# A one-core transformer block: the first half's attention ahead of all other work, the second half's scores behind two feed-forward units

## What is computed

```
h = layernorm(x) * (1 + ca) + sa
# latent attention: kv_latent = h W_to_kv^T (64), c = kv_latent W_compress^T (32), ch = layernorm(c)*gamma+beta
q, k, v = ch Wq^T, ch Wk^T, ch Wv^T          # one head of 32; rotary embedding on q and k
attn = softmax(causal(q k^T / sqrt(32)))      # 1024 x 1024
z = (attn v) W_comp2lat^T;  x = x + ga * (z (W_to_kv + W_out_res^T) + b_out)
h = layernorm(x) * (1 + cb) + sb
# gate, up: 2048 x 256, down: 256 x 2048, weights as packed 4-bit codes with one scale per 32
x = x + gb * ((gelu(h Wg^T) * (h Wu^T)) Wd^T)
```

## Time and profile before

| | us |
|---|---|
| median of 3 runs | 216.76 |
| lowest, highest | 214.21, 218.32 |
| the profiled execution, its own time | 217.49 |
| its span, first to last instruction | 215.5 |

### The profile page before, as it was taken

How to read it: one execution, slowest core, us unless ns; L and a number is a source line. 1 busy time by engine, 2 the same in 40 slices (tenths; PEclk the granted TensorE clock), 3 DMA queues, 4 the chain that set the end, 5 groups by cost and what they waited for, 6 DMA issues and landing times. The chain is left out here.

```text
span 215.5 us, 3087 instructions
## 1 busy us (share of the span) xinstructions
PE 198.3 (92%) x1064; PEld 159.3 (74%) x1064; DVE 142.7 (66%) x267; ACT 90.8 (42%) x151; POOL 59.4 (28%) x52
## 2 busy tenths in 40 slices
PE   7899998999769969989999999999899999999991
PEld 2496476574446848878898889887698889889891
DVE  0665995878799999999999844945832333323235
ACT  2011141642478526437535556354243542552420
POOL 4404043515152620200000000463342633624200
PEclk9885895599999999999999999999999999999998
DMA  5999675400000000000000000000200000000002
GB/s 177 324 349 235 193 230 196 171 4 3 0 0 2 0 0 3 2 0 0 3 0 0 3 0 0 0 0 5 97 2 0 0 0 0 3 0 0 0 0 97
DMA packets 5644, 11.30 MB, mean 52 GB/s; under 512 B 544, under 2 KB 2752, under 8 KB 5632
## 3 DMA queue, kind: packets, MB, share of 16 engines
q1 hardware_dynamic: 5216, 10.82, 16.0%
q10 hardware_dynamic: 416, 0.33, 0.6%
HBM read 10.09 MB, written 1.05 MB: 52 GB/s over the span
## 5 line engine op out<-in xcount | busy, mean ns | idle before, releaser
L866 PE MATMUL ps<-H,WS 128*128 128x512 f32 x384 | 94.7, 394 | 3.6 <-DVE wmod_sb L714 2.8
L866 PEld LDWEIGHTS ps<-H,WS 128*128 128x128 f32 x384 | 69.6, 188 | 18.9 <-DVE wmod_sb L714 4.3
L866 PEld LDWEIGHTS ps<-WS,IS 128*128 128x128 f32 x384 | 49.8, 191 | 3.8 <-issue 1.7
L866 PE MATMUL ps<-WS,IS 128*128 128x256 f32 x384 | 50.9, 283 | 1.1 <-DVE wmod_sb L714 0.9
L429 ACT ACTIVATE IS<-wmod_sb 128x512 fp32r<-128x512 f32 x32 | 20.3, 634 | 64.1 <-PE ps L866 41.0
L284 DVE TENSOR_TENSOR IS<-wmod_sb,IS 128x512 fp32r<-128x512 f32 x32 | 22.1, 690 | 26.6 <-ACT IS L429 25.0
L293 POOL TENSOR_TENSOR WS<-wbuf,WS 128x1024 fp32r<-128x1024 f32 x10 | 24.2, 2421 | 50.3 <-ACT WS L410 50.3
L714 DVE TENSOR_TENSOR wmod_sb<-ps,wmod_sb 128x512 f32<-128x512 f32 x32 | 22.0, 688 | 22.7 <-PE ps L866 20.7
L298 POOL TENSOR_TENSOR WS<-wbuf,WS 128x512 fp32r<-128x512 f32 x10 | 13.7, 1371 | 38.4 <-ACT WS L417 38.4
L423 ACT ACTIVATE wmod_sb<-ps 128x512 f32<-128x512 f32 x32 | 18.7, 586 | 6.2 <-PE ps L866 6.2
L866 PE MATMUL ps<-idle 128*128 128x512 bf16 x46 | 16.3, 502 | 1.3 <-POOL idle L487 1.3
(11 more groups left out here) (116 smaller groups left out, 203.3 us busy)
## 6 DMA issues: line engine op xcount, KB each, us to landing
wbuf<-packed SPq DMA_DIRECT2D x8, 384.0 KB, 17.7
wbuf<-scales SPq DMA_DIRECT2D x8, 384.0 KB
xres<-x SPq DMA_DIRECT2D x2, 512.0 KB, 6.2
wmod_sb<-wmod SPq DMA_DIRECT2D x1, 1024.0 KB, 11.0
out<-xres SPq DMA_DIRECT2D x4, 256.0 KB, 2.2
wmod_sb<-wmod SPq DMA_DIRECT2D x1, 512.0 KB, 7.1
rope_sb<-rope SPq DMA_DIRECT2D x1, 512.0 KB, 12.0
cst<-consts SPq DMA_DIRECT2D x1, 322.0 KB, 5.3
```

Of the source, the lines that this page charges most:

```text
L866: return pe.matmul(o, lhsT, rhs, start=start, stop=stop)
```

## The change

Every list of the front is written anew; what is computed stays the same.

- *Transfers.* x, with the identity matrix in front, comes as one tensor `head` laid out by partition, half 0 first; wmod likewise in two contiguous parts. SP's order is head half 0, wmod's first third, head half 1, the rest of wmod, consts, then rope half 0, group 0, rope half 1, group 1 and so on.
- *First LayerNorm.* `norm1` is gone. x is transposed raw; the mean is taken out in the weights (`wcm` minus 1/256 of its column sum, which PE computes in `weight_sum`), and 1/std is applied in `compress`, which also loses one step (eps sits in a 33rd column of `csq`).
- *Moved between engines.* `gamma_beta` and the sb and cb columns go from VectorE to ScalarE, the copy of xnT's second half too; both gate floors and `gab` go from VectorE to GpSimd; two of half 0's four `norm2` tiles go to ScalarE; staging of H for half 0 is split over both. `norm2` writes rows unpermuted, and `transpose2` reads with a step of 2.
- *Half 0.* Row scores come largest piece first, each with a bank of its own, and `max_rows(0)` follows each maximum. cb, sb and gb products, `project_c(1)` and `transpose_c(1)` are put in between on PE. The residual and the statistics alternate by tile; one reciprocal serves four tiles.
- *Feed-forward first.* `gate_up(0)` and `gate_up(1)` stand before half 1's row scores, `down(0)` behind the first four of these, `gate_up(2)` behind the other four, then half 1's key blocks without a unit in between, then `down(1)`. ScalarE does gelu of units 0 and 1 before half 1's exponentials. Unit 0, not unit 1, uses banks 2 and 3. `add_bias(1)` goes behind half 1's key blocks.
- *Fillers.* `stay_warm` has 10 matmuls at the start for 14, then 3, 2 and 4 in all that follow for 3, 4, 3, 2, 3, 3, 10 and 4.

```diff
@@ SP
+            sp.dma_start(head[:, 0:first], x[:, 0:first]).then_inc(x_in[0], 16)
+            sp.dma_start(wmod_flat[:, 0:KT * 2 * D], wmod[:, 0:KT * 2 * D]).then_inc(wmod_in[0], 16)
+            sp.dma_start(head[:, first:], x[:, first:]).then_inc(x_in[1], 16)
+            sp.dma_start(wmod_flat[:, KT * 2 * D:], wmod[:, KT * 2 * D:]).then_inc(wmod_in[1], 16)
             sp.dma_start(cst[:], consts).then_inc(cst_in, 16)
...
@@ ACT
             norm1_out(0)
             spread(0)
+            act.wait_ge(ga_done, 1)
+            act.activation(ga_b[:], bank(WO_B)[:, D:2 * D], ACT.Copy).then_inc(ga_out, 1)
+            norm1_out(1)
+            gamma_beta(0)
             v_high(0)
             qk_high(0)
             spread(1)
...
             exps(0, 0, HT)
+            split_d(0, 0)
+            out_high(0)
...
+            gamma_beta(1)
+            split_gu(0, 0)
+            v_high(1)
...
             spread(2)
+            norm2_h0((2, 3))
+            stage_h0()
             qk_high(1)
+            for n in range(2):
+                gelu(n, n, False)
+                inter_hi(n, n, False)
+                (split_gu, split_d)[n](1, 1)
             spread(3)
             max_rows(1)
+            exps(1, 0, 2 * HT)
...
@@ POOL
+            rsqrt(N_LN1)
             pool.wait_ge(a64_in, 16)
...
             rsqrt(N_LN1 + 1)
             rsqrt(N_LNC)
+            pool.wait_ge(ga_out, 1)
+            gate_floor(ga_b[:], ga_b[:]).then_inc(ga_ready, 1)
...
             add_bias(0)
             rsqrt(N_LNC + 1)
+            low_d(pool, 0, 0, 0)
             low_gu(pool, 0, 0, 0)
             rsqrt(N_LN2)
+            pool.wait_ge(gb_out, 1)
+            pool.wait_ge(wo_ready, 1)
+            gate_floor(gb_b[:], gb_b[:]).then_inc(gb_ready, 1)
+            low_gu(pool, 1, 1, 1)
+            low_d(pool, 1, 1, 1)
             for b in range(1, 2 * HT, 2):
                 probs_low(pool, 1, b, b + 1)
+            add_bias(1)
...
@@ DVE
             compress(0)
+            dve.tensor_copy(cbias[:], bank(SA_B)[:, DC:2 * DC]).then_inc(cbias_ready, 1)
+            decode(0, 0, 1)
             normc(0)
+            decode(0, 1, 3)
             rotate(0)
...
             split_qk(0)
+            row_max(0, 0, HT)
+            compress(1)
+            decode(0, 3)
...
+            aggregate(0, N_LN2)
             rotate(1)
...
+            norm2(0, (0, 1))
+            stage_h0()
             split_v(1)
             split_qk(1)
+            decode(1, 1, 3)
+            inter_full(0, 0, False)
+            inter_low(dve, 0, 0, False)
             decode(1, 3)
+            inter_full(1, 1, False)
+            inter_low(dve, 1, 1, False)
+            row_max(1, 0, HT)
+            decode_more(0, 1)
+            row_max(1, HT, len(pieces(1)))
+            for b in range(0, 2 * HT, 2):
+                decode_more(min(4, 1 + b // 2), min(4, 2 + b // 2))
+                probs_low(dve, 1, b, b + 1)
...
@@ PE
+            pe.wait_ge(ca_ready, 1)
+            weight_sum(bank(SUM_B, DC), M_CA).then_inc(sum_done, 1)
+            mod_columns(bank(SA_B, KT), SA, False).then_inc(moda_done, 1)
+            project_c(0, 0, HT)
...
+            transpose1(1)
+            stay_warm(0, 3)
             transpose_c(0)
+            project_c(1, 0, 2)
             project_qkv(0)
             stack_qk(0)
+            project_c(1, 2, HT)
+            scores(0, 0, HT)
+            max_rows(0)
             stay_warm(0, 2)
             key_scores(0, 0, 0)
             key_scores(0, 1, 1)
             key_scores(0, 2, 2)
+            pe.wait_ge(var_ready[N_LNC + 1], 1)
+            mod_columns(bank(MODB_B)[:, M_SB:M_SB + KT], SB, True)
             attend(0, 0, 0)
...
+            mod_columns(bank(MODB_B)[:, M_CB:M_CB + KT], CB, True).then_inc(modb_done, 1)
+            transpose_c(1)
+            output(0)
...
             project_qkv(1)
+            stay_warm(7, 4)
             stack_qk(1)
+            transpose2(0)
+            gate_up(0, 0, 0, 0, 0, first=True, later=False)
...
+            gate_up(1, 0, 0, 0, 1, later=False)
+            scores(1, 0, HT)
+            down(0, 0, 0, 0, 0, first=True)
+            scores(1, HT, len(pieces(1)))
+            gate_up(2, 1, 0, 1, 0)
             max_rows(1)
             for b, k in blocks(1):
                 key_scores(1, b, k)
                 if b >= 2:
                     attend(1, b - 2, k - 2)
...
+            down(1, 0, 0, 0, 1)
```

More of the change, by code:

```diff
@@ L65 @@
 EARLY = 2
-STEPS_AT_START = 5
-H0_BLOCK = 4
+STEPS_AT_START = 4
 H1_UNIT = 12
@@ new lines, in _ @@
+            dve.wait_ge(ca_ready, 1)
+            link(dve.tensor_tensor(wcm[:], wcc[:], mods[:, M_CA:M_CA + KT].unsqueeze(2).to_broadcast([P, KT, DC]),
+                                   ALU.mult))
+            dve.wait_ge(sum_done, 1)
+            dve.scalar_tensor_tensor(wcm[:], bank(SUM_B, DC).unsqueeze(1).to_broadcast([P, KT, DC]), -1.0 / D, wcm[:],
+                                     ALU.mult, ALU.add).then_inc(wcm_ready, 1)
+            dve.wait_ge(x_in[1], 16)
+            for i in range(HT, TILES):
+                bn(i)
@@ L797, in _ @@
-            probs_low(dve, 0, 3, HT)
-            decode(1, 2, 3)
-            out_stack(0)
-            rotate(1)
+            probs_low(dve, 0, 2, HT)
+            decode(1, 0, 1)
+            out_stack(0)
+            softmax_sums(0)
+            residual1(0, 0)
+            for i in range(HT):
+                if i < HT - 1:
+                    residual1(0, i + 1)
+                dve.wait_ge(x1_ready, i + 1)
+                bn(i)
+            aggregate(0, N_LN2)
+            rotate(1)
+            dve.wait_ge(rstd_ready[N_LN2], 1)
@@ new lines, in _ @@
+            inter_low(dve, 1, 1, False)
[5 more added lines that the diff above has]
+                probs_low(dve, 1, b, b + 1)
+            for n in range(2, UNITS + 2):
+                G = n // 2 + 1
+                if n == 2:
+                    dve.wait_ge(wgu_lo, 2)
+                    dve.wait_ge(wd_lo, 2)
+                    low_gu(dve, G, G % 2, G)
+                inter_full(n, n % 2)
+                if n == 2:
@@ L900, in _ @@
             pe.wait_ge(idle_ready, 1)
-            stay_warm(WC_B, 14)
+            stay_warm(WC_B, 10)
+            transpose1(0)
             pe.wait_ge(a64_in, 16)
@@ L1023, in gate_up @@
                     pe.wait_ge(wgu_lo, G + 1)
[L1024 to L1033 removed]
+                products = ((0, 0), (1, 0), (0, 1))
+                both = [(m, q) for m in range(2) for q in range(3)]
+                if first:
+                    both = [(m, q) for q in range(2) for m in range(2)] + [(m, 2) for m in range(2)]
+                for m, q in both:
+                    a, b = products[q]
+                    if later and q == 0:
+                        pe.wait_ge((gelu_done, inter_done)[m], n)
+                    if first and b and m == 0:
+                        pe.wait_ge(h_lo, 2 * (h + 1))
+                    for k in range(2):
+                        last = mm(bank(banks[m]), WS[:, par, a, k, m, P * e:P * (e + 1)], H[:, h, b, k, :],
+                                  q == k == 0, q == 2 and k == 1)
+                    if q == 2:
+                        last.then_inc((gate_done, up_done)[m], 1)
             def down(n, G, h, par, e, first=False, last=False, any_h=None):
@@ L1120, in _ @@
                 d = n - 2
-                down(d, d // 2, d // UNITS, d // 2 % 2, d % 2, first=d % UNITS == 0, last=d == UNITS - 1)
+                if d > 1:
+                    down(d, d // 2, d // UNITS, d // 2 % 2, d % 2, first=d % UNITS == 0, last=d == UNITS - 1)
             with pe.Fori(0, 3) as it:
```

497 lines of the change are left out of this document (233 added, 264 removed).

## The result

The changed kernel takes 224.02 us (median of 4 runs, 223.05 to 226.97); the kernel before, on the same chip, 216.70 (214.21 to 218.32). The ratio is 1.036, 95% interval 1.024 to 1.049: **slower**, outside the predicted range. The profiled execution took 223.54 us, its span is 221.7.

What follows compares the result with a forecast made beforehand. PE's and VectorE's chains to gate_up(12) were taken as the bound; PE's gave 4.75 us, VectorE's the deciding 4.2, so 217.5 - 4.2 = 213.3, less 0.7 for the median, rounded to 212.5 us; range 207.5 to 218.

Steps and rivals of the forecast that it cites:

- Part 1: Start to half 0's key scores: without LayerNorm's normalisations and with reordered transfers, done at 30.75, 6.1 us ahead.
- Part 2: Half 0's key scores to its output: output at 37.6, 8.6 us ahead, at the full clock.
- Part 3: Half 0's output to the first units: gate_up(0) at 46.9; units 0 and 1 done where unit 0 had 14 us to go.
- Part 4: Half 1's attention: 4.7 us PE wait, first exp at 68.0 (before 58.60), gate_up(4) at 83.2, 3.85 us ahead.
- the clock falls in the gap: Rival, chance 0.20: clock falls in Part 4's 4.7 us gap, gate_up(2) takes 5.5 instead of 2.8, gain 1.5, 215.3 us.
- Part 5: inter_full(3) to inter_full(11): VectorE takes 34.9 us, so gate_up(12) comes 4.2 us earlier.
- Slower: Rival, chance 0.11: clock stays low through half 1's attends, 219.1 us, or 222 with half 0 low too.
- hold between VectorE and GpSimd: In Part 4: exclusive lock for instructions with two SBUF inputs, not for PSUM readers; without it 1.5 us shorter.

Runs made afterwards that it cites:

- e1_decode_ahead: The changed kernel with decode steps 1 to 5 of the later groups done before half 1's first probability (STEPS_AT_START 6 for 4): 219.48 us.
- mended order: The changed kernel with decode two steps ahead and gelus of units 0 and 1 before split_gu(1,1); with fillers 215.13, repeated 0.994; without 218.66, repeated 1.014.
- w1_scores_first: The changed kernel with half 1's row scores ahead of the units, decode two steps ahead, gelus behind all exponentials, gb floor late: 216.09 us, ratio 0.991.
- w2_scores_first_trimmed: w1_scores_first with split_gu(1,1) behind half 1's exponentials, low_gu(1,1) on VectorE, gb floor back in the row maxima: 212.45 us, ratio 0.987.
- w4_scores_first_warm_early: w2_scores_first_trimmed plus eight fillers before max_rows(1) and five in the wait for the first attention bytes: 210.16 us, ratio 0.971.

## Why the prediction was wrong

The forecast and the profiled execution at the same points (us; the last column is how late the kernel was against the forecast):

| | forecast | measured | late |
|---|---|---|---|
| key scores of half 0 | 30.75 | 31.62 | 0.9 |
| output of half 0 | 37.6 | 39.56 | 2.0 |
| `gate_up(0)` | 46.9 | 50.25 | 3.4 |
| `gate_up(2)` | 62.3 | 65.73 | 3.4 |
| first exp of half 1 | 68.0 | 72.91 | 4.9 |
| `gate_up(4)` | 83.2 | 88.81 | 5.6 |
| `gate_up(12)` | 117.2 | 127.48 | 10.3 |

*Part 1 was right in its steps.* The first attention bytes landed 0.8 later than assumed, and `project_c(0)` ran at half clock, 3.60 us for my 2.6; of that 0.9 of lateness was left at the key scores.

*Part 2 and Part 3 were right in their steps and off in the clock.* The attends of half 0 at half clock I had priced (2.5 to 3.5 later) and not taken; by the output 1.1 of lateness came to the 0.9. `stack_qk(1)` took 3.47 us where I had the 1.98 of the earlier trace rows, nearly all of the next 1.4. GpSimd's floor of gb took five steps of 0.72 to 1.08 us, 4.6 in all for my 3; it ended at 49.8, before anything waited for it.

*Part 4 was right in its shape:* the gap of 4.7 us came as 4.41, VectorE's decodes and the split behind it in the order described, the two extra table loads with 1.28 each. Its term for `gate_up(2)` and for the attends was at the full clock, against 4.25 us and a clock of 0.66 measured. The rival "the clock falls in the gap" came true, but it priced one place, at 2.7 us, and 1.4 were lost there. The clock fell in at least three (at `stack_qk(1)`, in the gap, after the first attend). That the two falls after 60 us come with the waits is what the fillers show. For the first it is less sure: in e1_decode_ahead's profile `stack_qk(1)` stood behind the same wait of 0.88 us and took 1.96. The Trainium skill ("TensorE: Matmul & The Clock Gate", Part 1, "What's actually happening") has the throttled clock as the default and activity as what releases it; the runs agree for the holes after 60 us (1.00 with both filled, 0.50 to 0.66 behind them in the changed kernel), less for the fall at 12 us, which came with TensorE busy.

*Part 5 is the step that failed.* "The new order has the same 16 decode steps there ... I take 34.9" is a sum of VectorE's work, and as such it was good: VectorE was busy 34.18 us between `gate_up(4)` and `gate_up(12)`. But from `inter_full(3)` (88.72) to `inter_full(11)` (127.68), the stretch that the sum stood for, it was 38.96. What I took from it, that `gate_up(12)` follows within that time, was false: the stretch took 38.67 us, as VectorE has two decode steps fewer done at each unit than before, and TensorE and VectorE wait in turn for a split on ScalarE. With the table two steps ahead it takes 34.41. That is 4.3 of the 11.5 us between forecast and measurement, the largest single piece, and with nothing else it turns the forecast's gain of 4.2 to zero. It isn't the whole miss: with the table mended the time is 219.48, still above the range. The other 5.6 us had come by `gate_up(4)`, where Parts 1 to 4 priced TensorE at the full clock. By the rows above they are 0.9 at the start, 1.1 to half 0's output, 1.4 around `stack_qk(1)`, 1.5 from `gate_up(2)` to the first exp and 0.7 in half 1's attends; that the clock has most of them is my estimate from these durations, as no run holds the clock at 1.00 throughout.

*"Slower"* had a chance of 0.10, and by a mechanism (clock alone) that would have given 219 to 222. Decode ahead alone, with the clock as it fell, is 219.48, which is that rival's price, but partly by luck: it had 2.7 us at `gate_up(2)`, 1.4 at `down(1)` and 2.4 in half 1's attends, and the changed kernel lost 1.4, nothing (1.64 us, as at the full clock) and 0.7 there; the rest was lost in half 0 and at `stack_qk(1)`. The late table was in no rival.

*The hold between VectorE and GpSimd* was read rightly. In the changed kernel the subtraction at 76.04 took 1.28 us for 0.69 beside a GpSimd subtraction of 1.67, while four maxima, which read PSUM, took 1.80 at 62.84 beside a GpSimd instruction of 1.55.

*Does the order itself gain?* The mended order is about 1% below the kernel before at best, and only with fillers. Putting half 1's scores in front again, on the new front, gives 1% as it stands (0.991) and 3% (0.971) with the late waits taken away and two holes filled. Without the added fillers, and on the same chip, scores first has a ratio of 0.991 and the mended order 1.014. So the gain seems to lie in the front (half 0's output 6.6 us earlier) and in ending half 1's attention early: its first exp came at 59.5 in w1_scores_first and at 72.9 in the changed kernel, and with it the units behind. How much of it the new front is worth by itself isn't shown, and neither is what the same fillers would give the kernel before.

## What to carry to other kernels

Adding up an engine's busy time tells what the order could cost, not what it does: for each instruction that waits across engines compare how many steps ahead its producer stands in the old and in the new order, and take a lead of zero for a wait until a trace shows otherwise (here 3.85 us over four odd units, mended by standing two decode steps earlier; in the kernel before the same table gave one hole of 2.76 us and one of 0.49). Look at what stands behind a waiting instruction in its own engine's order: it was the gelu, not the split, that TensorE needed. And in a stage with several holes price the clock for all of them together: with one hole filled, the clock still fell at the next.

## What the runs showed of the hardware

- A granted clock of 0.50 came after waits of TensorE as short as 0.84 us at 7 us (changed kernel, `project_c(0)` 3.60 us) and 2.31 us at 72 us; after 1.88 us of waiting before `max_rows(1)` in w2_scores_first_trimmed it was 0.66 from 60 to 65. But not each time: in the kernel before waits of 0.97 and 1.58 us at 56 and 60 us left it at 1.00, and so did 1.75 us at 73 in w1_scores_first. The same wait of 0.88 us stood before `stack_qk(1)` in three kernels, which then took 3.47 us (changed kernel), 1.96 (e1_decode_ahead) and 3.60 (w4_scores_first_warm_early).
- The clock of one kernel falls at other places from execution to execution: the mended order without fillers had a mean clock of 0.80 over its first 60 us in one profile and 0.86 in the other, on another chip, and `down(0)` began at 59.56 and 56.60.
- GpSimd's one-input operations of 128x256 f32 took 0.85 to 1.17 us, its two-input ones 0.72 to 0.85: one input fewer was no gain.
